# Order of loads, first steps, layer change and last tile in a two-layer conditioned attention kernel

## The chip, the cores and the metric

One core of a Trainium2 chip runs the whole program. The time is the device time of one execution in microseconds (us); the kernel before was timed three times: median 972.3 us, 969.69 to 973.74. Beside these stands one execution that was recorded by the hardware profiler.

## The reference, cut to what matters

Two layers of the same shape, in float32, on x of 32 tiles of 128 rows by 512 (32 sequences of 128 positions). Layer 0 has 16 heads of 32, layer 1 has 8 heads of 64:

```python
xn = layernorm(x) * norm_scale + norm_bias
q, k, v = xn @ Wq + bq, xn @ Wk + bk, xn @ Wv + bv
k = masked(k); v = masked(v)
q = softmax(q, over the features of a head)
k = softmax(k, over the 128 positions)
att = k^T v                      # per sequence and head
y = q @ att
scale, shift = split(silu(cond) @ W_film + b_film)      # one row per sequence
h = layernorm(y) * (1 + scale) + shift
x = x + silu(h) @ Wo + bo
```

## The kernel before, in words

**Tiles and products.** A tile is one sequence. There are NT = 64 tile steps: tiles 0 to 31 are layer 0, tiles 32 to 63 layer 1, and x stays in SBUF (X) between the layers. Every float32 product with a weight is made of three products of rounded operands: each operand is split into a high part (XH, HH, WH, made by ScalarE as a rounding copy) and a low part (XL, HL, WL, made by VectorE or POOL as the difference). `split_product` (line 663) makes four chunks of three matmuls each. A weight's split is `split_high` and `split_low` (lines 503 and 256), per chunk of 128 rows.

**One step s** (the loops over SLOTS, one on each engine) works on four tiles at once: tile i = s gets its keys, values and queries; tile j = s-2 its query transpose, attention and mix; tile o = s-3 its transposed y, FiLM and output product; and x for step m = s+2 is brought into place. Each engine runs its own list of these stages in the order that its loop writes, and waits on semaphores; no engine reorders. So the order of the work is written by hand.

**x into place.** For the first two pairs of tiles (g < FIRST = 2) VectorE normalises (`norm_x`), TensorE transposes (`turn_x`), and ScalarE applies norm scale and bias into XF and rounds it to XH (`x_turned`). For later pairs ScalarE normalises into XN (its own `norm_x`), VectorE transposes 32x32 blocks (`turn_blocks`, to XS), and SP writes XS to HBM (`x_turned`) and reads it back in another order as XT (`place_x`, one write and four reads). The keys go the same way: VectorE takes the maximum and the differences (`keys`), ScalarE the exponentials (`exp_k`), VectorE divides and transposes blocks (`normalise_keys`, `turn_keys`, to KT), and `place_keys` on SP writes a pair of tiles to HBM (`k_turned`) and reads it back to EK, on which `attention` waits. EK has one buffer, so its reads wait for the attention of the pair before.

**SP's queue** issues nearly all DMAs in one order, waiting where its code says: in step s the stores, the mask, x or key placing, x loads, FiLM weights and weights. The x loads are XLOADS (line 152): eight loads, the last two of eight tiles (2 MB) each, both issued in step 3. Their place in X holds layer 0's FiLM weights until then. The FiLM product of the condition runs in FILM_SLOTS = steps 1, 2, 6, 9, 12 and 15 on TensorE (`conditioning`, then `conditioning_fold`).

**Layer change.** Layer 1's weights are loaded chunk by chunk into STAGE, split, and put in place of layer 0's. SPLIT_MID, SPLIT_LATE and SPLIT_END (line 229) say in which step and where in it each is split; w = 4, 5, 6, 7 are its key, value, query and output weights. LOW_ON_DVE (line 228) says which chunks VectorE takes; POOL takes the rest. DRAIN (line 236) is the order after the last step.

The functions that the diff touches:

## Time and profile before

| what | value |
|---|---|
| timed runs, median | 972.3 us (969.69 to 973.74) |
| the profiled execution, its own time | 965.67 us |
| its span | 963.6 us |
| TensorE busy | 907.3 us (94%) |
| VectorE busy | 731.0 us (76%) |
| ScalarE busy | 591.0 us (61%) |
| POOL busy | 446.5 us (46%) |
| mean granted TensorE clock | 0.98 |

TensorE's busy time is close to the span, so what counts is where it is not busy. The span is the time from the first to the last record of the profile; the execution's own time holds 2.1 us more around it. The granted clock is a share of full speed. In the rows a dash arrow `X<-Y` means that X is written from Y, and the bracket at the end of a row gives the idle time before it and what ended it.

### The profile page before, as it was taken

The page shows a single profiled execution, that of the slowest core. Times are in us where ns is not written, and L with a number is a line of the kernel's source. Part 1 is how long each engine was busy: PE and PEld are TensorE (multiplying, and loading weights), DVE is VectorE, ACT ScalarE, POOL GpSimd, SP SyncE. Part 2 cuts the span into 40 slices and gives each one's busy share as a digit, 9 for nine tenths or more (in the row PEclk, how much of TensorE's full clock was granted, in tenths as well). Part 3 has the DMA queues.
Part 4 walks back from the last instruction along what each step waited for, and adds up shares of the span by engine and source line. Part 5 has one row for each costly group of instructions (what it writes and reads, how often), then busy time and mean ns, then how long its engine had stood idle before and what let it go on. Part 6 is the DMA issues. An engine that isn't in the chain of part 4 may idle for free.

```text
span 963.6 us, 20376 instructions
## 1 busy us (share of the span) xinstructions
PE 907.3 (94%) x7069; PEld 773.0 (80%) x7069; DVE 731.0 (76%) x1347; ACT 591.0 (61%) x1445; POOL 446.5 (46%) x624
## 2 busy tenths in 40 slices
PE   4877899999999999999979999999999999999986
PEld 3555788888888888888868888888888888888874
DVE  6756577778688788888778888787888887877654
ACT  4336455756666677666766667666766666666634
POOL 3444344544545455445555645444554454443320
PEclk9989799999999999999989999999999999999998
DMA  8738223423232223222254222233333223223110
GB/s 299 276 93 284 72 72 116 132 100 110 72 117 75 90 94 94 94 77 84 73 169 138 101 81 93 95 106 92 117 115 114 86 93 104 99 89 111 67 67 33
DMA packets 69915, 105.84 MB, mean 110 GB/s; under 512 B 6687, under 2 KB 46743, under 8 KB 69815
## 3 DMA queue, kind: packets, MB, share of 16 engines
q1 hardware_dynamic: 69312, 104.10, 32.3%
q8 instruction: 57, 0.93, 0.4%
q10 hardware_dynamic: 502, 0.46, 0.2%
q14 instruction: 44, 0.35, 0.1%
HBM read 63.63 MB, written 40.89 MB: 108 GB/s over the span
## 4 chain that ended last, share of the span: by engine, by line
PE 78%; DMA 8%; ACT 4%; DVE 4%; issue 3%; SPq 2%; POOL 0%; ACTq 0%; DVEq 0%
PE PS L670 64%; PE PS L750 5%; DMA k_turned<-KT 4%; PE PS L736 3%; PE PS L710 3%; PE PS L718 2%; DMA EK<-k_turned 2%; ACT SK L518 1%; ACT Z L538 1%; DMA x_turned<-XS 1%; DMA STAGE<-in_wk 1%; SPq L324 1%; PE PS L784 1%; ACT XF L589 1%; SPq L312 1%
## 5 line engine op out<-in xcount | busy, mean ns | idle before, releaser
L524 ACT ACTIVATE YN<-YN,NBY,RSY 128x512 f32<-128x512 f32 x64 | 52.1, 815 | 266.4 <-POOL NBY L426 266.4
L670 PE MATMUL PS<-XH,WH_k 128*128 128x256 f32 x512 | 146.6, 286 | 6.1 <-DVE XL L906 4.8
L670 PE MATMUL PS<-XH,WL_k 128*128 128x256 f32 x512 | 146.2, 286 | 0.0
L670 PE MATMUL PS<-XL,WH_k 128*128 128x256 f32 x512 | 146.2, 285 | 0.0
L400 POOL TENSOR_SCALAR VEY<-MVY 128x1 f32<-128x1 f32 x64 | 14.9, 233 | 260.1 <-DVE MVY L993 259.8
L445 POOL TENSOR_TENSOR SQ<-SQ,QM 128x512 f32<-128x512 f32 x64 | 67.2, 1051 | 99.0 <-DVE QM L954 98.5
L670 PE MATMUL PS<-WH_o,HH 128*128 128x512 f32 x256 | 107.7, 421 | 5.4 <-DVE HL L1005 3.4
L670 PE MATMUL PS<-WH_q,XH 128*128 128x512 f32 x256 | 108.9, 425 | 2.9 <-DVE WL_q L261 2.9
L670 PEld LDWEIGHTS PS<-XH,WH_k 128*128 128x128 f32 x512 | 99.5, 194 | 9.7 <-ACT XH L596 5.2
L670 PE MATMUL PS<-WH_v,XH 128*128 128x512 f32 x256 | 106.2, 415 | 0.0
L670 PE MATMUL PS<-WL_o,HH 128*128 128x512 f32 x256 | 102.5, 401 | 0.0
L670 PE MATMUL PS<-WH_o,HL 128*128 128x512 f32 x256 | 102.2, 399 | 0.0
L670 PE MATMUL PS<-WL_q,XH 128*128 128x512 f32 x256 | 101.6, 397 | 0.0
L670 PEld LDWEIGHTS PS<-XL,WH_k 128*128 128x128 f32 x512 | 99.5, 194 | 2.6
L670 PE MATMUL PS<-WH_q,XL 128*128 128x512 f32 x256 | 101.4, 396 | 0.0
L670 PE MATMUL PS<-WH_v,XL 128*128 128x512 f32 x256 | 100.4, 392 | 0.0
L670 PE MATMUL PS<-WL_v,XH 128*128 128x512 f32 x256 | 99.5, 389 | 0.0
L670 PEld LDWEIGHTS PS<-XH,WL_k 128*128 128x128 f32 x512 | 99.5, 194 | 0.0
L518 ACT ACTIVATE SK<-SK,KN 128x128 f32<-128x128 f32 x256 | 98.7, 387 | 0.0
L538 ACT ACTIVATE Z<-PS,FC,FA 128x128 f32<-128x128 f32 x256 | 96.2, 463 | 2.2 <-PE PS L718 2.2
L438 POOL TENSOR_TENSOR X<-X,BB 128x512 f32<-128x512 f32 x64 | 84.7, 1323 | 4.9
L454 POOL TENSOR_TENSOR XL<-XF,XH 128x512 fp32r<-128x512 f32 x60 | 77.6, 1294 | 19.7 <-ACT XH L596 19.7
(124 smaller groups left out, 2206.8 us busy)
## 6 DMA issues: line engine op xcount, KB each, us to landing
k_turned<-KT SPq DMA_DIRECT2D x32, 512.0 KB, 2.7
EK<-k_turned SPq DMA_DIRECT2D x128, 128.0 KB, 2.8
x_turned<-XS SPq DMA_DIRECT2D x30, 512.0 KB, 2.6
XT<-x_turned SPq DMA_DIRECT2D x120, 128.0 KB, 2.8
out_x<-X SPq DMA_DIRECT2D x32, 256.0 KB, 2.1
X<-in_film SPq DMA_DIRECT2D x2, 2048.0 KB, 17.1
X<-in_x SPq DMA_DIRECT2D x2, 2048.0 KB, 11.8
STAGE<-in_film SPq DMA_DIRECT2D x4, 1024.0 KB, 8.1
```

The costliest lines, as they stand in the source:

```text
L400: eng.tensor_scalar(plus, var, EPS, None, ALU.add).then_inc(pool_own, 1)
L438: eng.tensor_tensor(X[:, b, :], X[:, b, :], BB[:, 2, :], ALU.add).then_inc(pool_bo, 1)
L445: eng.tensor_tensor(sq, sq, QM[:, 0:D // w].unsqueeze(2).to_broadcast([P, D // w, w]), ALU.subtract)\
L454: eng.tensor_tensor(XL[g % 2][:, dst, :], XF[:, :, :], XH[g % 2][:, dst, :].bitcast(F32), ALU.subtract).then_inc(pool_xl, 1)
L518: e = eng.activation(SK[:, p, a, :], SK[:, p, a, :], ACT.Exp, bias=KN[:, t, cc:cc + 1], accum_out=SE[:, a:a + 1])
L524: eng.activation(YN[:, :], YN[:, :], ACT.Identity, bias=NBY[:, :], scale=RSY[:, :]).then_inc(act_yn, 1)
L538: z = eng.activation(Z[:, c * P:c * P + P], PS[:, B_TY, c * P:c * P + P], ACT.Identity, bias=FC[l][:, c, b:b + 1], scale=FA[l][:, c, b:b + 1])
L670: mm = eng.matmul(dst, left[a](c), right[b](c), start=(c == 0 and a + b == 0), stop=(c == C - 1 and a == 1))
L710: mm = eng.transpose(bank(B_TQ, c * P, P), SQ[j % 2][:, c * P:c * P + P], ident[:, :])
L718: mm = eng.transpose(bank(B_TY, c * P, P), YN[:, c * P:c * P + P], ident[:, :])
L736: mm = eng.matmul(PS[f:f + 32, B_ATT, c * P + a:c * P + a + w], vs if l == 0 else ks, ks if l == 0 else vs, start=True, stop=True, tile_po ...
L750: mm = eng.matmul(bank(B_Y + c // 2, (c % 2) * W, W), EQ[:, c * P:c * P + P], ATT[:, c // 2, (c % 2) * W:(c % 2 + 1) * W], start=True, sto ...
```

## The change: what it does

- XLOADS: tiles 16 to 31 come in eight loads of two tiles, one in each of steps 3 to 10, and these loads and the FiLM loads are issued behind `place_keys`. In step 1 x is placed before the keys.
- XF has two buffers, and the second half of a pair uses a PSUM bank of its own (B_Y) for its transposes; XN's halves are apart too. The waits of `x_turned`, `turn_x` and `norm_x` are loosened accordingly.
- Start: ScalarE turns both halves of x before it splits weights; keys(0) waits chunk by chunk; x of steps 2 and 3 is made in step 0; VectorE takes three of four chunks of the query weights (w = 2); `start_cond` moves behind values(0).
- Layer change: w = 4 is split at the end of step 31, w = 5 first in step 32, w = 6 at the end of step 32; queries(32) come last in step 32 on TensorE; the chunks are shared out anew.
- End: keys of tile 63 are made, normalised and placed in step 62.

```diff
@@ -79,7 +79,7 @@
         XT = sb("XT", [P, Q, 2, C, 32])
-        XF = sb("XF", [P, 2, PAIR])
+        XF = [sb(f"XF{n}", [P, 2, PAIR]) for n in range(2)]
         XH = [sb(f"XH{n}", [P, C, PAIR], F32R) for n in range(2)]
@@ -147,9 +147,10 @@
         B_ATT = B_XK
-        XLOADS = [(0, 1), (1, 1), (2, 2), (4, 4), (8, 4), (12, 4), (16, 8), (24, 8)]
+        B_X = [B_XK, B_Y]
+        XLOADS = [(0, 1), (1, 1), (2, 2), (4, 4), (8, 4), (12, 4)] + [(n, 2) for n in range(16, B, 2)]
         ld_x = [sem(f"ld_x{n}") for n in range(len(XLOADS))]
@@ -217,6 +218,10 @@
+        def keys_at(s):
+            return [NT - 1] if s == NT - 2 else []
         def block_turn_at(s):
@@ -225,8 +230,8 @@
-        LOW_ON_DVE = [range(C), range(C), [3], [], range(2), range(2, C), range(C), []]
-        SPLIT_MID, SPLIT_LATE, SPLIT_END = {31: [4], 32: [6]}, {31: [5]}, {1: [3], 34: [7]}
+        LOW_ON_DVE = [range(C), range(C), [1, 2, 3], [], range(2), range(3), range(2), []]
+        SPLIT_FIRST, SPLIT_LAST, SPLIT_END = {B: [5]}, {B - 1: [4], B: [6]}, {1: [3], 34: [7]}
         LAST_USE = {4: pe_k, 5: pe_v, 6: pe_q, 7: pe_o}
@@ -352,20 +357,8 @@
                     load_mask(eng, s // 2 + 1)
-                for g in block_turn_at(s) if s > 1 else []:
+                for g in block_turn_at(s):
                     place_x(g)
-                if s == 3:
-                    eng.wait_ge(pe_film, 2)
-                    load_x(6)
-                    load_x(7)
-                    wait_split(3)
-                for n in range(2, 6):
-                    if s == FILM_SLOTS[n - 1] + 1:
-                        eng.wait_ge(pe_film, n)
-                        load_film(n)
-                if s == FILM_SLOTS[-1] + 1:
-                    eng.wait_ge(pe_film, 6)
-                    load_w(4)
                 if s == B - 1:
@@ -375,10 +368,22 @@
                     load_w(7)
-                if s % 2 == 1:
+                if s % 2 == 1 and s < NT - 2:
                     place_keys(s // 2)
-                for g in block_turn_at(s) if s == 1 else []:
-                    place_x(g)
+                if s == NT - 2:
+                    place_keys(NT // 2 - 1)
+                if s == 3:
+                    eng.wait_ge(pe_film, 2)
+                    wait_split(3)
+                if 3 <= s < 11:
+                    load_x(s + 3)
+                for n in range(2, 6):
+                    if s == FILM_SLOTS[n - 1] + 1:
+                        eng.wait_ge(pe_film, n)
+                        load_film(n)
+                if s == FILM_SLOTS[-1] + 1:
+                    eng.wait_ge(pe_film, 6)
+                    load_w(4)
             for b in range(B - 4, B):
@@ -451,7 +456,7 @@
                 dst = slice(2 * p, 2 * p + 2)
-                eng.tensor_tensor(XL[g % 2][:, dst, :], XF[:, :, :], XH[g % 2][:, dst, :].bitcast(F32),
+                eng.tensor_tensor(XL[g % 2][:, dst, :], XF[p][:, :, :], XH[g % 2][:, dst, :].bitcast(F32),
                                   ALU.subtract).then_inc(pool_xl, 1)
@@ -473,6 +478,8 @@
                     queries(s - 1)
+                for w in SPLIT_FIRST.get(s, []):
+                    split_low(eng, w, low_on_pool(w))
                 if 2 * FIRST <= s + 2 < NSTEP:
@@ -480,7 +487,7 @@
                     mask_of_keys((s + 1) // 2)
-                for w in SPLIT_MID.get(s, []) + SPLIT_LATE.get(s, []):
+                for w in SPLIT_LAST.get(s, []):
                     split_low(eng, w, low_on_pool(w))
@@ -579,21 +586,20 @@
                     eng.wait_ge(dve_vec, 1)
-                wait_x_low(eng, m)
-                eng.wait_ge(act_xh, m)
+                wait_x_low(eng, m - 1)
                 for cc in range(2):
                     if g < FIRST:
-                        src = PS[:, B_XK, cc * PAIR:(cc + 1) * PAIR].rearrange("p (t q n) -> p t q n", t=2, q=Q)
+                        src = PS[:, B_X[p], cc * PAIR:(cc + 1) * PAIR].rearrange("p (t q n) -> p t q n", t=2, q=Q)
                     else:
                         src = XT[:, :, :, 2 * p + cc, :].rearrange("p q t n -> p t q n")
-                    f = eng.activation(XF[:, cc, :].rearrange("p (t q n) -> p t q n", t=2, q=Q), src, ACT.Identity,
+                    f = eng.activation(XF[p][:, cc, :].rearrange("p (t q n) -> p t q n", t=2, q=Q), src, ACT.Identity,
                                        bias=vec(l, "norm_bias", 2 * p + cc, 1),
...
                     eng.wait_ge(pe_q, 2 * g - 2)
-                eng.activation(XH[g % 2][:, 2 * p:2 * p + 2, :], XF[:, :, :], ACT.Copy).then_inc(act_xh, 1)
+                eng.activation(XH[g % 2][:, 2 * p:2 * p + 2, :], XF[p][:, :, :], ACT.Copy).then_inc(act_xh, 1)
@@ -608,9 +614,8 @@
             x_turned(0)
-            split_high(0, range(2))
             x_turned(1)
-            split_high(0, range(2, C))
+            split_high(0)
             split_high(1)
@@ -620,26 +625,34 @@
                     norm_y(o)
+                for w in SPLIT_FIRST.get(s, []):
+                    split_high(w)
                 if s in FILM_SLOTS:
                     conditioning_sums(FILM_SLOTS.index(s))
-                if m < NSTEP:
+                if s < 2:
+                    exp_k(i)
+                if s != 1 and m < NSTEP:
                     x_turned(m)
+                if s == 0:
+                    x_turned(m + 1)
                 if 0 <= j:
...
                     film(o)
-                exp_k(i)
+                if 2 <= s < NT - 1:
+                    exp_k(i)
                 if 0 <= j:
                     heads(j)
-                for w in SPLIT_MID.get(s, []):
-                    split_high(w)
                 if 0 <= o:
...
                 values(i)
-                if s > 0:
-                    for n in (norm_at(0) if s == 1 else []) + norm_at(s):
-                        norm_x(n)
-                for w in SPLIT_LATE.get(s, []) + SPLIT_END.get(s, []):
+                for w in SPLIT_LAST.get(s, []):
+                    split_high(w)
+                for n in keys_at(s):
+                    exp_k(n)
+                for n in norm_at(s):
+                    norm_x(n)
+                for w in SPLIT_END.get(s, []):
                     split_high(w)
@@ -666,6 +679,9 @@
                         eng.wait_ge(low_w[fresh][c], 1)
+                    if fresh == 0 and c % 2 == 0:
+                        eng.wait_ge(act_xh, c // 2 + 1)
+                        eng.wait_ge(dve_xl, c // 2 + 1)
                     for a, b in ((0, 0), (0, 1), (1, 0)):
@@ -675,8 +691,9 @@
                 l = i // B
-                eng.wait_ge(act_xh, 2 * g + 2)
-                wait_x_low(eng, 2 * g + 2)
+                if i > 0:
+                    eng.wait_ge(act_xh, 2 * g + 2)
+                    wait_x_low(eng, 2 * g + 2)
                 eng.wait_ge(dve_ka, i)
@@ -743,6 +760,8 @@
                 eng.wait_ge(dve_yr, j)
+                if j == 0:
+                    eng.wait_ge(act_xf, 2 * FIRST)
                 if j >= B:
@@ -763,11 +782,14 @@
             def turn_x(m):
+                g, p = divmod(m, 2)
                 eng.wait_ge(dve_xn, m + 1)
-                eng.wait_ge(act_xf, m)
+                if m >= 2:
+                    eng.wait_ge(act_xf, m - 1)
                 for cc in range(2):
                     for t in range(2):
-                        mm = eng.transpose(bank(B_XK, cc * PAIR + t * T, T), XN[:, t, cc * P:cc * P + P], ident[:, :])
+                        f = (2 * p + cc) * P
+                        mm = eng.transpose(bank(B_X[p], cc * PAIR + t * T, T), XN[:, t, f:f + P], ident[:, :])
                 mm.then_inc(pe_a, 1)
@@ -802,20 +824,19 @@
                 i, j, o, m = s, s - 2, s - 3, s + 2
-                if 0 <= i < NT:
+                if s < NT - 1:
                     keys(i)
...
                     conditioning(FILM_SLOTS.index(s))
-                if 0 <= j < NT:
+                if 0 <= j:
                     turn_queries(j)
-                if 0 <= o < NT:
+                if 0 <= o:
                     turn_y(o)
-                if 0 <= i < NT:
-                    values(i)
-                if 0 <= j < NT:
+                values(i)
+                for n in keys_at(s):
+                    keys(n)
+                if 0 <= j:
                     attention(j)
-                if 1 <= s and m < 2 * FIRST:
-                    turn_x(m)
                 if s == 0:
@@ -824,11 +845,11 @@
                     conditioning_fold(FILM_SLOTS.index(s))
-                if 0 <= i < NT:
+                if s != B:
                     queries(i)
                 if s == 0:
-                    turn_x(m)
-                if s == 0:
+                    turn_x(2)
+                    turn_x(3)
@@ -837,10 +858,12 @@
                     mm.then_inc(pe_cond, 1)
-                if 0 <= j < NT:
+                if 0 <= j:
                     mix(j)
-                if 0 <= o < NT:
+                if 0 <= o:
                     output(o)
+                if s == B:
+                    queries(i)
             for stage, n in DRAIN:
@@ -879,11 +902,13 @@
                 eng.wait_ge(pool_x, 2 * g + 2)
-                eng.wait_ge(pe_a, m)
+                if g > 0:
+                    eng.wait_ge(pe_a, m - 1)
                 for t in range(2):
...
                     r = n % RING
-                    ins = eng.tensor_scalar(XN[:, t, 0:2 * P], X[:, n % B, 2 * p * P:2 * (p + 1) * P], MVX[:, r, 0:1],
+                    f = slice(2 * p * P, 2 * (p + 1) * P)
+                    ins = eng.tensor_scalar(XN[:, t, f], X[:, n % B, f], MVX[:, r, 0:1],
                                             RSX[:, r:r + 1], ALU.subtract, ALU.mult)
@@ -903,7 +928,7 @@
                 dst = slice(2 * p, 2 * p + 2)
-                eng.tensor_tensor(XL[g % 2][:, dst, :], XF[:, :, :], XH[g % 2][:, dst, :].bitcast(F32),
+                eng.tensor_tensor(XL[g % 2][:, dst, :], XF[p][:, :, :], XH[g % 2][:, dst, :].bitcast(F32),
                                   ALU.subtract).then_inc(dve_xl, 1)
@@ -1082,57 +1107,65 @@
             x_low(0)
-            split_low(eng, 0, range(2))
             x_low(1)
-            split_low(eng, 0, range(2, C))
+            split_low(eng, 0, range(C))
             start_masks()
...
             stat_x(3)
-            start_cond()
+            split_low(eng, 2, LOW_ON_DVE[2])
+            norm_x(2)
+            norm_x(3)
             for s in SLOTS:
...
                     queries(s - 1)
-                if 0 < s and m < 2 * FIRST:
-                    norm_x(m)
+                for w in SPLIT_FIRST.get(s, []):
+                    split_low(eng, w, LOW_ON_DVE[w])
                 for g in block_turn_at(s) if s > 1 else []:
                     turn_blocks(g)
-                keys(i)
+                if s < NT - 1:
+                    keys(i)
                 if s == 0:
-                    split_low(eng, 2, LOW_ON_DVE[2])
                     values(i)
-                    norm_x(m)
                     start_valid()
+                    start_cond()
+                    x_low(2)
+                    normalise_keys(i)
                     start_count()
+                    x_low(3)
                 for n in stats_at(s):
...
                     h_mul(o)
-                for w in SPLIT_MID.get(s, []):
-                    split_low(eng, w, LOW_ON_DVE[w])
                 if s > 0:
...
                     second_ones()
-                normalise_keys(i)
+                if 0 < s < NT - 1:
+                    normalise_keys(i)
                 if 0 <= o:
                     h_low(o)
-                if m < 2 * FIRST:
-                    x_low(m)
+                for w in SPLIT_LAST.get(s, []):
+                    split_low(eng, w, LOW_ON_DVE[w])
                 if s in FILM_SLOTS:
                     conditioning(FILM_SLOTS.index(s))
-                turn_keys(i)
+                if s < NT - 1:
+                    turn_keys(i)
+                for n in keys_at(s):
+                    keys(n)
                 if 0 <= j:
                     mixed(j)
+                for n in keys_at(s):
+                    normalise_keys(n)
+                    turn_keys(n)
                 if s == 1:
...
                     turn_blocks(g)
-                for w in SPLIT_LATE.get(s, []) + SPLIT_END.get(s, []):
+                for w in SPLIT_END.get(s, []):
                     split_low(eng, w, LOW_ON_DVE[w])
...
```

## Rows read from the trace of the kernel before

**Rows 1.** Stretches view, a step each: bounds, length, busy times, clock, DMA.

```profile
core 0: us, PE busy (x) PEld busy (x) DVE busy (x) ACT busy (x) POOL busy (x), PEclk, DMA share, GB/s
322.18:335.71 13.53, 13.53 (x110) 11.68 (x108) 10.06 (x19) 8.93 (x22) 5.84 (x10) 1.00 0.21 51
...
29.34:46.79 17.45, 13.80 (x78) 9.43 (x77) 11.59 (x25) 8.60 (x26) 8.24 (x13) 0.90 0.72 265
...
46.79:67.08 20.29, 14.36 (x117) 11.16 (x117) 10.37 (x19) 9.40 (x22) 9.95 (x10) 0.88 0.37 111
...
67.08:83.41 16.33, 14.95 (x111) 12.69 (x111) 14.69 (x28) 8.81 (x22) 7.72 (x13) 0.94 0.45 143
...
83.41:110.20 26.79, 16.34 (x110) 13.73 (x108) 10.14 (x19) 9.03 (x22) 5.88 (x10) 0.75 0.56 193
...
470.98:489.73 18.75, 15.32 (x110) 12.88 (x109) 15.15 (x25) 13.61 (x31) 14.73 (x16) 0.91 0.45 155
...
489.73:507.38 17.65, 15.05 (x110) 12.75 (x108) 12.19 (x23) 11.19 (x26) 5.17 (x8) 0.90 0.40 127
```

**Rows 2.** The waits of TensorE: line, waited for, us in total, times, longest.

```profile
PE PS L736 <- DMA EK<-k_turned: 16.5, 5, 10.5
```

**Rows 3.** Timeline of TensorE: start, length, what, idle before it.

```profile
34.88 3.62 PE L784 MATMUL PS<-X,CT 128*32 128x512 f32 x16 [2.40 <-DVE SQ L950]
...
46.79 0.36 PE L670 MATMUL PS<-XH,WH_k 128*128 128x256 f32 x1 [1.24 <-issue]
...
65.33 2.10 PE L750 MATMUL PS<-ATT,EQ 128*128 128x132 f32 x8 [5.51 <-issue]
...
100.50 0.66 PE L736 MATMUL PS<-EK,VV 128*32 128x32 f32 x32 [10.45 <-DMA EK<-k_turned]
...
160.36 0.46 PE L736 MATMUL PS<-EK,VV 128*32 128x32 f32 x32 [1.35 <-DMA EK<-k_turned]
...
245.89 0.46 PE L736 MATMUL PS<-EK,VV 128*32 128x32 f32 x32 [0.77 <-DMA EK<-k_turned]
...
485.30 0.60 PE L670 MATMUL PS<-WH_o,HH 128*128 128x512 f32 x1 [3.43 <-DVE HL L1005]
...
499.36 0.77 PE L670 MATMUL PS<-WH_q,XH 128*128 128x512 f32 x1 [2.60 <-DVE WL_q L261]
...
937.64 0.65 PE L736 MATMUL PS<-VV,EK 128*32 128x64 f32 x32 [3.21 <-DMA EK<-k_turned]
...
943.55 2.10 PE L750 MATMUL PS<-ATT,EQ 128*128 128x132 f32 x8 [2.75 <-ACT ATT L557]
```

**Rows 4.** Chain of waits in step 3, issuing queue: start, length, what.

```profile
79.26 3.91 SPq L293
...
83.22 12.96 DMA k_turned<-KT
```

**Rows 5.** List of DMA issues: how many, KB each, us to landing.

```profile
k_turned<-KT SPq DMA_DIRECT2D x32, 512.0 KB, 2.7
...
EK<-k_turned SPq DMA_DIRECT2D x128, 128.0 KB, 2.8
```

**Rows 6.** The timeline of ScalarE, POOL and VectorE in the first steps.

```profile
12.07 1.15 ACT L509 ACTIVATE WH_k<-STAGE 128x512 fp32r<-128x512 f32 x2 [1.83 <-DMA STAGE<-in_wk]
...
19.62 4.22 POOL L261 TENSOR_TENSOR WL_q<-X,WH_q 128x512 fp32r<-128x512 f32 x3 [10.00 <-ACT WH_q L509]
...
21.05 1.64 DVE L1061 SCALAR_TENSOR_TENSOR KT<-Z,KT 32x512 f32<-32x512 f32 x1
...
76.81 0.69 DVE L998 SCALAR_TENSOR_TENSOR H<-H,Z 128x512 f32<-128x512 f32 x1 [0.44 <-ACT H L543]
```

**Rows 7.** The timeline of POOL at the layer change.

```profile
481.71 2.94 POOL L261 TENSOR_TENSOR WL_k<-STAGE,WH_k 128x512 fp32r<-128x512 f32 x2
```

**Rows 8.** The timeline of TensorE and ScalarE in step 62.

```profile
916.40 1.06 PE L750 MATMUL PS<-ATT,EQ 128*128 128x132 f32 x8
...
920.79 0.81 ACT L524 ACTIVATE YN<-YN,NBY,RSY 128x512 f32<-128x512 f32 x1 [5.11 <-POOL NBY L426]
...
923.40 0.60 PE L718 MATMUL PS<-ident,YN 128*128 128x128 f32 x4
```

More of the change, by code:

```diff
@@ L1175 @@
         arrays[f"film{l}"] = g["film"]
-    nc = bacc.Bacc("TRN2", target_bir_lowering=False, num_devices=1, dynamic_dma_scratch_size=4096)
+    nc = bacc.Bacc("TRN2", target_bir_lowering=False, num_devices=1, dynamic_dma_scratch_size=2048)
     arrays = {f"in_{k}": np.ascontiguousarray(v) for k, v in arrays.items()}
```

## Prediction

> **What bounds the kernel now.** I read the stretches view by step first. A step is the time from one tile's first key matmul to the next one's. In an undisturbed step of layer 0 TensorE is busy 13.53 us out of 13.53, so nothing that other engines save there can show; only lost TensorE time can be won back [rows 1]. Against those 13.53 us, steps 1 to 4 take 17.45, 20.29, 16.33 and 26.79 us, and the two steps at the layer change 18.75 and 17.65 us [rows 1]. Next came TensorE's waits. Waiting for the read-back of placed keys (EK) costs 16.5 us in five places, 10.5 of it in one [rows 2]. Then each idle stretch by time, with what ended it [rows 3]: the 10.45 us before the attention of step 4, 5.51 us before a mix in step 2, 3.43 and 2.60 us at the layer change, 3.21 and 2.75 us at the end. Last, the chain of waits around the largest: SP issues two x loads (eight tiles, 2 MB each), a 1 MB FiLM load at 79.26, and only at 83.22 the key write, which takes 12.96 us to land [rows 4]; the read-back that follows it ended the wait at 100.50. The usual landing times are 2.7 us for the write and 2.8 us for a read-back part [rows 5].
>
> **Step 4 (late x loads behind the placing): 13.3 us.** The two x loads and the FiLM load of step 3 move behind the key write and read-back. Key write to attention was 83.22 to 100.50, 17.3 us. With nothing ahead it is 2.7 (write) + 1.8 (four issues at about 0.43) + 2.8 (landing) = 7.3 us [rows 5]. By the order of VectorE's work, KT should be turned about 8.5 us before the attention is due, so I expect 1 us of slack and no wait. Step 4 falls from 26.79 to 13.53, or 13.3 us: the 10.45 us wait and 2.8 us that the same work took longer at the lower clock (mean granted 0.75 in that step) [rows 1, 3]. Cover gone means a stall of up to 4 us: bounds 9 to 13.3. The eight pieces add six issues on SP of 0.43 us each; their data is first read in step 11 and SP has idle time in each step, so I cost them at nothing; if placings wait behind them see the rivals.
>
> **Steps 8 and 14: 2.1 us.** FiLM loads issued in steps 7 and 13 now also come after the placing; they preceded EK waits of 1.35 and 0.77 us [rows 3]. Bounds 0 and 2.1. The wait of 0.7 us in step 34, the rest of the five, follows the load of layer 1's output weights, whose place ahead of the keys is unchanged; it stays.
>
> **First steps: 3.3 us.** I followed each queue in the new order.
> Step 0: the second half of x no longer waits for the first (own XF, own bank) nor stands behind two weight chunks, and each weight chunk releases its own three matmuls. WH_k starts at 12.07 [rows 6]; plus 0.6 and 0.7 the first matmul goes at about 13.5, 2.1 us earlier than 15.62. Taking two of POOL's three WL_q chunks (4.22 us for three [rows 6]) to VectorE ends the queries 3 us earlier. None of it is carried on: VectorE still reaches keys(0) at 24.4, since two statistics, three WL_q chunks and two normalisations stand in front, and TensorE's keys(1) stands behind start_cond, at about 27.1 + 1.4 + 0.7 = 29.2, against 29.34 [rows 1].
> start_cond took 1.64 us for its first instruction while POOL ran; the same form on 128 partitions takes 0.69 elsewhere [rows 6]. It is now clear of POOL's chunk, so I take 0.69 twice, 1.4; at the old price, bound 3.4, keys(1) would be 2.0 us later.
> The Trainium skill (GPSIMD Engine Reference, Specifications) says that GpSimd and VectorE share SBUF interfaces and contend when a VectorE instruction has two SBUF inputs. By it the sum is the 1.4 one; without it, the 3.4 one.
> Step 1: the FiLM matmuls waited until 34.88 for VectorE's queries(0) [rows 3]. The new queue puts an x_low, the count and both statistics before it: about 35.7, 0.8 us lost. Then turn_x(3) (0.45 us) is gone, and so is the 1.24 us wait for the XL of step 2 [rows 3]: keys(2) at 46.0, 0.8 ahead.
> Step 2: XN is ready early, so XS is turned at 46.8. SP now writes x first: 46.8 + 2.7 + 1.8 = 51.3 for the key write, + 2.7 + 1.8 + 2.8 = 58.6 for EK. The attention, due at 54.2, waits 4.4 us; ScalarE has x in time, so the 5.51 us wait of the mix is replaced by it, not removed. The rest of the step (5.1 us) plus 1.7 us of lower clock puts keys(3) at 65.4, 1.7 ahead of 67.08.
> Step 3: no cold start, but YN after the late mix still comes a microsecond late: 14.7 to 14.9 against 16.33, 1.4 to 1.6 more. Sum 3.3. Below, if start_cond and VectorE's queue run later, -1; above, if step 2's wait goes as well, 8.
>
> **Layer change: 3.6 us.** In step 31 ScalarE's four WH_k chunks move behind h_high, which removes the 3.43 us wait for HL [rows 3]. POOL's two WL_k chunks (2.94 us [rows 7]) end near 485.0, in time for the fourth chunk of keys(32), which starts at 484.7 instead of 489.73: 5.0 won. In step 32 two waits are new. The WL_v split stands first: with POOL's chunk after its queries, values(32) ends at 492.5, 1 us late. The key write still stands behind four value-weight loads and a bias on SP (485.9, as before), so EK lands at 494.7 and the attention waits 2.2 us. ScalarE then owes a split, x, exp, FiLM and exp before the copy of ATT (496.9), so the mix waits 1.7 us more and the output 0.4 us. Queries(32), now last, find WL_q ready (2.60 us wait [rows 3] gone). Keys(33) at 503.8 against 507.38: 3.6. Both steps at 13.53 would give 9.3 [rows 1]; ScalarE or POOL 4 to 5 us later than I reckon would give -1.
>
> **End: 1.0 us.** keys(63) in step 62 lets EK be written early; the read-back waits only for the attention of step 61, so the 3.21 us wait goes [rows 3]. What is late next is POOL's queries(63). Moving 2.9 us of keys from between the mix and the next turn_y to before the mix costs: mix at 916.40, YN at 920.79 + 0.81 = 921.6, 5.2 us later; a mix at 919.3 gives YN at 924.5 where TensorE is there at 923.4: 1.1 lost [rows 8]. With all that the last mix starts at 942.9 instead of 943.55, 0.6 won. It runs at the low clock now (2.10 us [rows 3]); I add 0.4 for a shorter cold part. Bounds -1 and 4.
>
> **Sum**: 13.3 + 2.1 + 3.3 + 3.6 + 1.0 = 23.3 us. The profiled execution had a span of 963.6 and a time of 965.7, so it would come to 940.3 and 942.4. The median of the timed runs is 972.3, 6.6 above it; I subtract from that: 949.0.
>
> **Rivals.**
> (A) The forecast, 949.0, own range 943 to 955: chance 0.55.
> (B) The layer change is hidden fully: 9.3 instead of 3.6, so 943.3; all upper bounds together (13.3 + 2.1 + 8 + 9.3 + 4 = 36.7) give 935.6. For it: TensorE alone needs 13.53 a step. Against: the key write behind the value weights. Chance 0.2.
> (C) The reordering is a wash and only the DMA order pays: 15.4, so 956.9. For it: VectorE is busy 14.69 us of step 3's 16.33 and 15.15 of step 31's 18.75 [rows 1], and each reorder adds work before something. Chance 0.15.
> (D) It doesn't do what it says: each piece delays a placing as a FiLM load did, 1.35 us in eight steps, 10.8, and the 2.1 isn't won either: 972.3 - 23.3 + 12.9 = 961.9. Against: each piece is issued after the read-back and has most of a step to land. Chance 0.06.
> (E) The other side. In steps 3, 5, 7 and 9 a piece, twice with a FiLM load, and then the next piece follow the read-back at once. If the engines share out between them, at the 2.6 us a MB that the key write's 12.96 us behind 5 MB shows [rows 4], 2 MB make EK some 5 us late, and each such stall costs 2.8 us of low clock more: 4 x 7.8 = 31, so 980. It decides from 3.0 us late in each of the four, 4 x 5.8 = 23.3. Against: the FiLM load of step 10 is already issued behind a read-back, and step 10 shows no wait. Chance 0.04.
> For (E) the Trainium skill (DMA: Bandwidth & Descriptors, Queues, rings and completion order) says that descriptors of one issuing engine's ring are consumed in ring order, and round-robin is between rings; all these come from SP. By that rule the later loads would not slow the read-back; by sharing, the time would be 980.
>
> **How the numbers follow.** Faster by over 0.5% (4.9 us, about what a measurement of this kernel can tell): A, B, C, D, 0.96 less a little for all of them shrinking: 0.95. Same 0.02, slower 0.03. The range leaves out (D), (E) and the far end of (B): 938 to 958.
>
> **What would show it.** Right: step 4 at 13.5 to 14.5 us and no EK wait over 1 us in steps 4 to 14; the first key matmul at 13.5 and keys(1) still at 29; an EK wait of about 4 us in step 2 in place of the mix's; keys(32) 13.7 us after keys(31), then a 19 us step with EK and ATT waits; no EK wait after step 63. Wrong: step 4 over 17 us, an EK wait in each even step up to 10, or both steps of the layer change at 13.6.

## The result, and the profile after

The changed kernel took 944.75 us, median of 4 runs (942.48 to 946.47), beside 971.0 us (964.75 to 973.74) for the kernel before: a ratio of 0.9737, interval 0.9684 to 0.979, so 2.7% faster. The profiled execution has a span of 943.2 us and a time of 944.95, so between the two profiles 20.4 us went. When both were run again the ratio was 0.978 (0.9754 to 0.9806). The kernel before had medians of 967.25 to 968.59 us in three later sets of nine runs, so its four runs here lie high, and a gain of 22 to 24 us, 2.2 to 2.5%, is the better figure.

A stretch's bounds are the first key matmuls of two tiles. The stretches by step of the changed kernel (stretch, its length, busy time and instructions of PE, PEld, DVE, ACT and POOL, granted clock, DMA share, GB/s): steps 1 to 4, 8 and 14, then 31, 32 and 34, and the end from step 62 on. They answer to [rows 1].

```profile
28.79:43.59 14.80, 13.82 (x73) 11.20 (x73) 12.73 (x28) 7.09 (x17) 8.28 (x13) 0.82 0.88 323
43.59:65.78 22.19, 16.64 (x117) 12.99 (x116) 10.67 (x19) 9.14 (x21) 10.04 (x10) 0.77 0.32 101
65.78:81.06 15.28, 14.08 (x111) 11.82 (x110) 13.42 (x24) 8.81 (x22) 7.62 (x12) 1.00 0.32 105
81.06:94.59 13.53, 13.53 (x110) 11.68 (x108) 10.08 (x19) 8.93 (x22) 5.93 (x10) 1.00 0.65 205
136.75:150.75 14.00, 13.59 (x109) 11.68 (x108) 10.06 (x19) 8.93 (x22) 5.87 (x10) 1.00 0.62 200
221.90:235.41 13.51, 13.51 (x110) 11.66 (x109) 10.08 (x19) 8.92 (x22) 5.90 (x10) 1.00 0.41 128
453.55:467.08 13.53, 13.53 (x110) 11.68 (x108) 12.54 (x22) 11.01 (x26) 9.63 (x11) 1.00 0.34 105
467.08:488.35 21.27, 16.89 (x110) 13.94 (x108) 14.94 (x27) 14.15 (x31) 11.24 (x16) 0.84 0.58 175
501.87:515.58 13.71, 13.71 (x110) 11.83 (x108) 10.16 (x23) 8.93 (x22) 5.79 (x10) 1.00 0.17 50
886.49:943.20 56.71, 44.15 (x353) 36.21 (x351) 29.57 (x54) 26.01 (x61) 11.04 (x19) 0.96 0.17 56
```

Step 4 is an undisturbed step now: 13.53 against 26.79. Step 31 is whole too, and step 32 is longer than the 17.65 it took. Step 2 grew from 20.29 to 22.19. The waits of TensorE (us in total, times, longest) answer to [rows 2]:

```profile
PE PS L753 <- DMA EK<-k_turned: 9.1, 3, 5.6
PE PS L735 <- ACT YN L531: 4.6, 5, 1.5
PE PS L769 <- ACT ATT L564: 2.8, 1, 2.8
```

EK fell from 16.5 us in five waits to 9.1 in three. The idle stretches of TensorE (start, length, instruction, idle time before it and its releaser) say where, beside [rows 3]:

```profile
13.48 0.55 PE L686 MATMUL PS<-XH,WH_k 128*128 128x256 f32 x1 [3.86 <-DVE WL_k L266]
35.26 1.92 PE L806 MATMUL PS<-X,CT 128*32 128x512 f32 x16 [0.98 <-DVE SQ L975]
57.38 0.66 PE L753 MATMUL PS<-EK,VV 128*32 128x32 f32 x32 [5.55 <-DMA EK<-k_turned]
143.82 0.46 PE L753 MATMUL PS<-EK,VV 128*32 128x32 f32 x32 [0.41 <-DMA EK<-k_turned]
477.87 0.61 PE L753 MATMUL PS<-EK,VV 128*32 128x32 f32 x32 [3.13 <-DMA EK<-k_turned]
905.19 0.66 PE L735 MATMUL PS<-ident,YN 128*128 128x128 f32 x4 [1.45 <-ACT YN L531]
919.13 0.66 PE L727 MATMUL PS<-ident,SQ 128*128 128x128 f32 x4 [1.23 <-POOL SQ L450]
924.03 1.14 PE L769 MATMUL PS<-ATT,EQ 128*128 128x132 f32 x8 [2.75 <-ACT ATT L564]
```

The waits of [rows 3] at 100.50, 245.89, 485.30, 499.36 and 937.64 have no counterpart. In their place stand 5.55 us before the attention of step 2 (where the mix had waited 5.51), 3.13 us before that of step 32, and short ones at the end (the 2.75 us before the last mix was there before).

### The profile page after: what moved, and what is told of

The parts are those of the page before. It is cut to its first block, busy times and chain, and to the rows that moved or that the text cites. A ratio compares the mean times of both kernels' runs of the same rounds, so it can differ in the third digit from the quotient of the medians.

```text
span 943.2 us, 20349 instructions
## 1 busy us (share of the span) xinstructions
PE 904.5 (96%) x7069; PEld 772.6 (82%) x7069; DVE 729.0 (77%) x1348; ACT 591.2 (63%) x1445; POOL 444.1 (47%) x623
## 4 chain that ended last, share of the span: by engine, by line
PE 87%; DMA 4%; DVE 3%; ACT 2%; issue 2%; SPq 1%; POOL 1%; DVEq 0%; ACTq 0%; POOLq 0%
PE PS L686 71%; PE PS L769 6%; PE PS L753 3%; PE PS L735 3%; PE PS L727 3%; DMA X<-in_x 1%; DMA k_turned<-KT 1%; DMA EK<-k_turned 1%; PE PS L806 1%; ACT Z L545 1%; ACT SK L525 0%; PE PS L815 0%; SPq L329 0%; SPq L288 0%; ACT YN L531 0%
## 5 line engine op out<-in xcount | busy, mean ns | idle before, releaser
L459 POOL TENSOR_TENSOR XL<-XF,XH 128x512 fp32r<-128x512 f32 x60 | 77.6, 1293 | 15.8 <-ACT XH L602 15.6
```

What stands on the lines that cost most here:

```text
L459: eng.tensor_tensor(XL[g % 2][:, dst, :], XF[p][:, :, :], XH[g % 2][:, dst, :].bitcast(F32), ALU.subtract).then_inc(pool_xl, 1)
```

## The experiments

In the expectations "changed" is the changed kernel. Each diff is against it unless it says otherwise. The kernel before, run beside them, had a median of 968.59 (e1 to e4), 967.76 (e5 to e8) and 967.25 us (e11, e12), nine runs each.

**e1: the DMA order alone.** The kernel before, with one part of the change. (One line that belongs to no part differs too between the kernel before and the changed one with all its versions, and in e1: `dynamic_dma_scratch_size` is 2048 instead of 4096. No run varies it alone. In e3, with 2048, the wait of step 4 is there, and in e1 the start, the layer change and the end take what they take in the three profiles of the kernel before, within 0.2 us of one of them each, so nothing points to it.)

```diff
-XLOADS = [..., (16, 8), (24, 8)]
+XLOADS = [...] + [(n, 2) for n in range(16, B, 2)]
-                # x loads, FiLM loads and load_w(4) between place_x and place_keys
                 place_keys(s // 2)
+                # ... the same ones here; one load_x a step
```

> The kernel before, with only the order of loads changed: eight loads of two tiles in steps 3 to 10, and these and the FiLM loads behind the key placing; step 1, the start, the layer change and the end stay as before. Theory (the late loads alone remove the stall of step 4): step 4 falls from 26.8 to 13.5 us, steps 8 and 14 give 1.8 to 2.1 more, the rest stays; 15.0 to 15.4 us less than the kernel before in the profile, span about 948. Rival (parts help each other: the stall goes only since the first steps also end earlier): step 4 keeps an EK wait of 2 us or more, and the gain is under 11 us.

It took 950.32 us: ratio 0.9815 (0.9789 to 0.984), span 948.0. Its stretches of steps 4, 31 and 32:

```profile
81.33:94.84 13.51, 13.51 (x109) 11.67 (x108) 10.08 (x19) 8.92 (x22) 5.87 (x10) 1.00 0.65 205
453.62:471.99 18.37, 14.95 (x110) 12.62 (x108) 15.23 (x25) 13.58 (x30) 14.55 (x15) 0.93 0.48 158
471.99:490.10 18.11, 15.51 (x109) 13.17 (x108) 12.12 (x23) 11.33 (x26) 5.45 (x9) 0.88 0.39 124
```

The theory's span of about 948 came, and no EK wait is left in step 4. Step 4 is mended with the start, the layer change and the end as they were. So this part carries 18.3 of the gain in medians, and the rest of the change 5 to 6 us.

**e2: two loads of eight tiles, behind the placing.**

```diff
-XLOADS = [...] + [(n, 2) for n in range(16, B, 2)]
+XLOADS = [..., (16, 8), (24, 8)]
-                if 3 <= s < 11:
-                    load_x(s + 3)
+                if s == 3:
+                    load_x(6)
+                    load_x(7)
```

> The changed kernel, but tiles 16 to 31 come again in two loads of eight tiles, both issued in step 3 behind the key placing. Theory (the place in the queue counts, the size doesn't): no EK wait in step 4 and a span within 1 us of 943.2, or up to 3 us more if the 5 MB (two loads and FiLM) are still moving when step 5 writes x. Rival (DMAs of one queue share the engines, so what is issued behind a read-back slows it): EK lands late in step 4, an EK wait of 5 us or more there, span 950 or more.

It took 944.85 us: 0.9758 (0.9737 to 0.978). Steps 4 and 5, and then SP's queue (issue time, its length), in two fences:

```profile
82.22:95.72 13.50, 13.50 (x109) 11.66 (x108) 10.08 (x19) 8.92 (x22) 5.87 (x10) 1.00 0.88 279
95.72:109.25 13.53, 13.53 (x109) 11.69 (x108) 11.91 (x21) 8.92 (x22) 7.65 (x11) 1.00 0.78 269
```

```profile
82.56 1.73 SPq L329 DMA_DIRECT2D EK<-k_turned  x4
84.46 1.02 SPq L283 DMA_DIRECT2D X<-in_x  x2
85.52 4.69 SPq L298 DMA_DIRECT2D STAGE<-in_film  x1
```

Four megabytes issued within 2 us of the read-back leave both steps undisturbed: its four parts landed in a median of 2.9 us, as against 2.8 as a rule [rows 5]. The place in the queue counts, not the size of the loads, and rival (E), that the engines share out between them, falls.

**e3: the loads ahead again, the rest of the change kept.**

```diff
-XLOADS = [...] + [(n, 2) for n in range(16, B, 2)]
+XLOADS = [..., (16, 8), (24, 8)]
                     place_x(g)
+                # load_x(6), load_x(7), the FiLM loads and load_w(4) here
                 ...
                 place_keys(s // 2)
-                # ... and no longer here
```

> The changed kernel with the loads where they were: two loads of eight tiles and the FiLM load ahead of the key placing of step 3, the later FiLM loads ahead of theirs; all else of the change kept. Theory (terms add up): the 13.3 us of step 4 and the 1.8 of steps 8 and 14 come back, span 943.2 + 15 = 958. Rival (the other parts hide part of the stall, or the stall grows since keys are ready earlier while the loads take as long): a span of 952 or less, or 961 or more.

It took 963.41 us: 0.9945 (0.9924 to 0.9965), span 960.4. The attention of steps 4, 8 and 14:

```profile
98.14 0.66 PE L753 MATMUL PS<-EK,VV 128*32 128x32 f32 x32 [10.76 <-DMA EK<-k_turned]
158.38 0.46 PE L753 MATMUL PS<-EK,VV 128*32 128x32 f32 x32 [2.62 <-DMA EK<-k_turned]
245.58 0.60 PE L753 MATMUL PS<-EK,VV 128*32 128x32 f32 x32 [2.45 <-DMA EK<-k_turned]
```

The wait of 10.45 us is back, and step 4 takes 26.22 us. The span lies between the theory's 958 and the rival's 961: step 4 cost 12.7 us (13.3 in the theory), but steps 8 and 14 cost 6.3 instead of 1.8, with waits longer than the 1.35 and 0.77 of [rows 3]. That is no effect of the other parts, since the kernel before has waits of 2.02 and 2.56 there in e9: their price is no constant.

**e4: the key write parted from its read-back,** and put ahead of the x placing in step 1 and of the value weights in step 31.

```diff
+            def write_keys(g): ...      # the wait for KT and the write
-            def place_keys(g):
+            def place_keys(g, write=True):
+                if s == 1:
+                    write_keys(0)
                 place_x(g)
                 if s == B - 1:
+                    write_keys(s // 2)
                     load_w(5)
-                    place_keys(s // 2)
+                    place_keys(s // 2, s not in (1, 31))
```

> The changed kernel with the write of the keys parted from their read-back on the issuing queue in two steps: in step 1 the key write goes ahead of the placing of x, in step 31 ahead of the load of the value weights; the read-backs stay where they are. Theory (both remaining EK waits come from the write standing behind other DMAs, and each costs its wait and then low clock): step 2 falls from 22.2 to about 16.5 us, the wait of 5.6 us going to 1 or less and its low clock with it; step 32 from 21.3 to about 17 us; span about 933. Rival (another wait takes the place of each: ScalarE's copy of ATT in step 32, x for ScalarE in step 2): the EK waits go but an ATT wait of 2 us or more stands behind them, and the span stays over 939.

It took 941.79 us: 0.9726 (0.9701 to 0.9751), span 938.8. Steps 1, 2 and 32, and TensorE's waits in them:

```profile
28.21:45.00 16.79, 14.56 (x75) 11.05 (x74) 12.71 (x29) 7.33 (x17) 7.81 (x13) 0.80 0.82 301
45.00:61.81 16.81, 14.78 (x117) 11.43 (x116) 10.66 (x18) 9.14 (x21) 10.04 (x10) 0.90 0.43 134
463.40:484.32 20.92, 16.42 (x109) 13.39 (x108) 15.20 (x27) 14.95 (x33) 12.09 (x16) 0.84 0.62 188
```

```profile
55.26 0.46 PE L761 MATMUL PS<-EK,VV 128*32 128x32 f32 x32 [2.03 <-DMA EK<-k_turned]
472.90 0.66 PE L761 MATMUL PS<-EK,VV 128*32 128x32 f32 x32 [1.09 <-DMA EK<-k_turned]
475.68 2.10 PE L777 MATMUL PS<-ATT,EQ 128*128 128x132 f32 x8 [2.12 <-issue]
```

In step 2 the EK wait falls by 3.5 us and the step by 5.4, of which step 1 gives back 2.0 in this execution. In a second one (e12) step 1 took 14.81 us and step 2 18.81: the two together 33.6 in both, against 37.0 and 38.6 in the changed kernel's two profiles. In step 32 the EK wait falls by 2.0 and the step only by 0.35 (in e12 by nothing, 21.38 us): the mix now waits 2.12 us, where it had waited 0.75. By ScalarE's timeline its copy of ATT ends just before the mix starts. So the theory held for steps 1 and 2 and the rival for step 32.

**e5: the start as before.** Steps 0 and 1 get back x behind the keys, the order of splits and turns, the place of `start_cond`, and the query weights' chunks; the buffers stay two. The diff is cut.

```diff
-LOW_ON_DVE[2] = [1, 2, 3]
+LOW_ON_DVE[2] = [3]
-                if s != 1 and m < NSTEP: x_turned(m)
-                if s == 0: x_turned(m + 1)
+                if m < NSTEP: x_turned(m)
+                if s == 1: turn_x(3)        # first on TensorE in step 1
```

> The changed kernel with the first steps as in the kernel before: order of steps 0 and 1 on all engines, x behind the keys in step 1, shares of the query weights. Late loads, layer change and last tile as changed. Theory (the first steps are worth little or nothing; most of the 2.35 us by which step 4 starts earlier was that one conditioning product ran at the full clock): step 4 starts within 1.5 us of the changed kernel's 81.1, span 943 to 945, timed the same within 2 us. Rival (the 3.3 us of the prediction are real): step 4 starts at 83.4 or later and the kernel is 2.3 to 3.3 us slower than the changed one.

It took 944.4 us: 0.9756 (0.9732 to 0.9781), span 942.5. Steps 1, 2 and 3:

```profile
28.86:44.61 15.75, 12.08 (x78) 9.16 (x77) 11.59 (x25) 8.59 (x26) 8.26 (x13) 1.00 0.81 299
44.61:64.24 19.63, 14.34 (x116) 11.16 (x117) 10.36 (x19) 9.41 (x22) 9.95 (x10) 0.90 0.37 114
64.24:80.58 16.34, 15.46 (x110) 13.17 (x110) 14.70 (x28) 8.81 (x22) 7.73 (x13) 0.91 0.28 98
```

Step 4 starts at 80.58, no later than in the changed kernel (81.06), and the medians agree within 0.8 us: the theory was right. The reordered start is worth nothing that this run could show. The kernel before itself starts step 4 at 81.43 in e9, so if the first steps gained anything, the second buffers, which e5 keeps, may have given it; no run has them alone.

**e6: the layer change as before.**

```diff
-LOW_ON_DVE[5], LOW_ON_DVE[6] = range(3), range(2)
+LOW_ON_DVE[5], LOW_ON_DVE[6] = range(2, C), range(C)
-SPLIT_FIRST, SPLIT_LAST = {B: [5]}, {B - 1: [4], B: [6]}
+SPLIT_MID, SPLIT_LATE = {31: [4], 32: [6]}, {31: [5]}
-                if s == B:
-                    queries(i)              # last in step 32
```

> The changed kernel with the weight splits of steps 31 and 32 and the queries of tile 32 in the places of before. Theory (what step 31 wins, step 32 gives back in waits for EK and ATT and in low clock): steps 31 and 32 take 36.4 together against 34.8, and step 34 some 14.5 against 13.7; 1.6 to 2.4 us slower than the changed kernel. Rival (with the keys ready early anyway the new order costs nothing extra): 3.6 us slower or more.

It took 949.3 us: 0.9803 (0.9779 to 0.9826), 4.5 us over the changed kernel's median. Steps 31, 32 and 34:

```profile
453.60:472.25 18.65, 15.24 (x109) 12.89 (x108) 15.13 (x25) 13.60 (x30) 14.72 (x16) 0.91 0.48 156
472.25:491.71 19.46, 16.18 (x110) 13.63 (x108) 12.20 (x23) 11.54 (x26) 5.18 (x8) 0.82 0.37 115
505.23:520.57 15.34, 13.79 (x110) 11.83 (x108) 10.20 (x23) 9.04 (x22) 5.80 (x10) 1.00 0.32 98
```

Steps 31 and 32 take 38.11 instead of 34.80 (the theory had 36.4), and step 34 gets back the wait that I had forecast to stay in it. The loss of 4.1 to 4.5 us, by which of the changed kernel's medians is taken, is the rival's "3.6 or more".

**e7: the keys of tile 63 in their own step.**

```diff
-            return [NT - 1] if s == NT - 2 else []
+            return []
-                if s < NT - 1: keys(i)
+                keys(i)
 ...              # exp_k, normalise_keys, turn_keys and place_keys likewise
```

> The changed kernel with the keys of tile 63 in step 63 as before. Theory (the 3.2 us EK wait comes back, the 1.45 us wait for YN in step 63 goes, and the rest of the end follows POOL's queries and the low clock): 0.5 to 1 us slower, span 943.7 to 944.2. Rival (the early keys help by the whole wait): 3 us slower. Third (early keys cost more than they save): faster by 0.5 us or more.

It took 947.01 us: 0.9792 (0.976 to 0.9824); in the profile the end takes 57.48 instead of 56.71. The span is 0.9 us over the changed kernel's, as in the theory; the median is 1.8 to 2.3 over it, one of the four runs being at 952.29, so the size stays between theory and rival. The end's stretch, and the wait that is back, in two fences:

```profile
886.62:944.10 57.48, 45.10 (x353) 37.95 (x351) 29.64 (x54) 25.78 (x61) 10.74 (x19) 0.94 0.16 56
```

```profile
917.94 0.98 PE L751 MATMUL PS<-VV,EK 128*32 128x64 f32 x32 [3.25 <-DMA EK<-k_turned]
```

**e8: x for step 34 behind the split in step 32,** on top of e4, with VectorE taking all four low chunks of w = 6.

```diff
-LOW_ON_DVE[6] = range(2)
+LOW_ON_DVE[6] = range(C)
-                if s != 1 and m < NSTEP:
+                if s not in (1, B) and m < NSTEP:
                     x_turned(m)
                     split_high(w)
+                if s == B:
+                    x_turned(m)
```

> The kernel of the parted key writes (steps 1 and 31), and in step 32 ScalarE turns x of tile 34 behind the split of the query weights instead of ahead of the exponentials, and VectorE takes all four low chunks of the query weights. Theory (ScalarE's queue ahead of the ATT copy is what bounds step 32 once EK is early): ATT is copied 1.5 us earlier, the mix waits 1 us or less, step 32 falls from 20.9 to about 18 us, span 935.5 to 937. Rival (VectorE takes over as the bound, with the low chunks, the keys and the mix of the same step): the ATT wait shrinks but queries(32) or the YN of step 33 waits instead, step 32 and 33 together within 1 us of 34.4.

It took 941.87 us: 0.9731 (0.9707 to 0.9755), no better than e4. Within step 32:

```profile
470.00:476.40 6.40, 3.71 (x44) 2.46 (x45) 5.86 (x13) 5.97 (x19) 1.28 (x1) 0.95 1.09 296
476.40:481.00 4.60, 4.59 (x15) 4.01 (x16) 3.58 (x7) 4.27 (x8) 0.00 (x0) 0.50 0.37 133
```

```profile
470.43 0.47 PE L696 MATMUL PS<-WH_v,XH 128*128 128x512 f32 x1 [1.43 <-DVE WL_v L266]
476.41 2.10 PE L779 MATMUL PS<-ATT,EQ 128*128 128x132 f32 x8 [1.13 <-issue]
```

The wait for ATT falls from 2.12 to 1.13 us, nearly as forecast, but the first value matmul waits 1.43 us for WL_v instead of 0.51, and what follows runs at 0.50 of the clock. Nothing that the edit moves stands ahead of that wait. ScalarE's own row shows that it stood idle 0.97 us for the load of the value weights before its first chunk, which it had not in e4; and in e12, e4's kernel again, the wait for WL_v is 1.00 us.

```profile
468.86 1.88 ACT L524 ACTIVATE WH_v<-STAGE 128x512 fp32r<-128x512 f32 x3 [0.97 <-DMA STAGE<-in_wv]
```

Steps 32 and 33 take 34.54 us together, the number of the rival; its cause, VectorE as the bound, isn't shown. In the first stretch ScalarE is busy 5.97 and VectorE 5.86 us of 6.40, so neither has room there.

**e9, e10: the kernel before, twice more,** for how much its own steps vary; no edit.

> The kernel before once more, profiled, to see where its timed runs, 962 to 974 us, differ from its first profiled one (965.7, span 963.6). Theory (the waits behind loads vary from run to run): the EK waits of steps 4, 8, 14 and 34, 10.5, 1.4, 0.8 and 0.7 us in the first profile, come out 3 us or more apart from these in sum when the span is 966 or more; steps 17 to 30 at 13.53 us as ever. Rival (the low clock in the first steps and the layer change varies instead): these waits agree within 1 us and steps 0 to 3 or 31 to 32 carry the difference.

> The same kernel a third time, with the same expectations, since one more profile may fall on either end of its spread.

They took 968.44 and 966.66 us (spans 966.7 and 964.9). Step 4 took 25.83 and 26.74 us. Steps 8, 14 and 34 of the first of the two:

```profile
149.42:165.04 15.62, 13.60 (x110) 11.68 (x108) 10.11 (x19) 9.02 (x22) 5.80 (x10) 1.00 0.22 64
236.15:253.84 17.69, 15.13 (x109) 12.84 (x108) 10.13 (x19) 9.03 (x22) 5.88 (x10) 0.90 0.26 85
522.06:537.35 15.29, 13.83 (x109) 11.83 (x108) 10.21 (x23) 9.03 (x22) 5.80 (x10) 1.00 0.29 98
```

The same steps took 14.99, 14.34 and 14.53 us in the first profile. Most undisturbed steps repeat to 0.03 us; those behind a load don't. The EK waits of steps 4, 8, 14 and 34 sum to 16.9 us in e9, 3.6 more than in the first profile, with a span of 966.7: the theory held.

**e11, e12: the changed kernel and e4's kernel again,** side by side.

> The changed kernel once more, on the chip and in the rounds of the next run. Theory (its first profile is typical): step 4 starts at 80.5 to 82.5, steps 31 and 32 take 34.3 to 35.1, 13 and 14 take 27.4, median 943 to 946. Rival: one of these lies outside, and the parts as read from one profile are off by as much.

> The parted key writes once more, beside the changed kernel. Theory (the gain is the 5.4 us of step 2 less some low clock in step 1): 2.5 to 5 us faster than the changed kernel in the same rounds. Rival (low clock elsewhere gives it all back): within 1 us of it.

They took 945.17 (944.1 to 946.25; 0.978, 0.9754 to 0.9806) and 943.39 us (940.95 to 943.9; 0.9762, 0.9736 to 0.9787). All four numbers expected of e11 came: step 4 starts at 82.29, steps 31 and 32 take 34.92, steps 13 and 14 27.35. The parted key write gains 1.8 us in medians (3.0 when e4 is set against the changed kernel's 944.75) and 5.3 between the two profiled spans, 944.5 and 939.2. The gain of medians lies between e12's theory (2.5 to 5) and its rival (within 1), and the two ratios' intervals overlap: it is the fastest version run, by too little to be sure of its size.

## Why the prediction was right

949.0 was forecast and 944.75 measured, inside the range. Of the rivals, (C) gave 956.9 and (B) 943.3, which is nearer the measured time than the forecast is; the rows below tell them apart where the time alone can't. Each line of the table takes all profiled executions with the old arrangement of that part, and all with the new one (for the first steps the start of step 4, for the others their lengths). In the three lines with six executions, the versions with the key write moved (e4, e8, e12) are left out:

| part | old | new | gain | forecast |
|---|---|---|---|---|
| step 4 | 26.4 (4 executions) | 13.5 (10) | 12.9 | 13.3 |
| steps 8, 13, 14 | 45.4 (4) | 41.4 (10) | 4.0 | 2.1 |
| first steps | 82.0 (5) | 81.4 (6) | 0.6 | 3.3 |
| steps 31 + 32 | 37.1 (5) | 34.6 (6) | 2.4 | 3.6 |
| step 34 | 14.8 (5) | 13.7 (9) | 1.1 | 0 |
| end from step 62 | 57.8 (5) | 56.5 (6) | 1.3 | 1.0 |
| sum | | | 22.3 | 23.3 |

The medians of e11 and of the kernel before beside it are 22.1 us apart. The sum came close in part by luck: the first steps gave 2.7 us less than forecast, steps 8 and 14 gave 1.9 more, and step 34 gave 1.1 that I had not counted.

**Step 4: right in size and cause.** e1 takes the wait away with no other part of the change, e3 brings it back with all others kept, and the changed kernel shows no EK wait over 0.5 us in steps 4 to 14 in either profile.

On the queue, the Trainium skill (DMA: Bandwidth & Descriptors, Queues, rings and completion order) says that on each DMA engine the descriptors of a ring are consumed in ring order. e2 agrees: 4 MB right behind the read-back cost it nothing, where 5 MB right ahead of the key write cost 10 us [rows 4].

**First steps: the term that was mis-sized, 0.6 instead of 3.3 us.** Every wait came where the working had put it: the first key matmul at 13.48 (13.5 forecast), keys(1) at 28.79 (29.2), and an EK wait in step 2 in place of the mix's. The step that failed is the one that priced what follows this wait: "the rest of the step (5.1 us) plus 1.7 us of lower clock". Two stretches of step 2, the wait and what comes after it:

```profile
51.83:57.38 5.55, 0.00 (x1) 0.01 (x1) 1.56 (x3) 3.74 (x12) 4.10 (x6) 0.76 0.49 138
57.38:65.78 8.40, 8.40 (x60) 7.18 (x61) 1.72 (x5) 1.91 (x3) 0.85 (x1) 0.55 0.06 10
```

The rest took 8.40 us and not 6.8 (8.23 in e11), at a mean granted clock of 0.55, which is nearly all of it at 1.2 GHz. The old wait stood at the step's end, before the mix, with 1.75 us of step 2 behind it [rows 1, 3]; the new one has queries and mix behind it. The wait was also 5.55 and not 4.4 us, and step 3 took 15.28 and not 14.7 to 14.9. In e11 keys(2) start at 45.33, 0.7 us earlier than the forecast's 46.0, and then step 2 takes 21.70 where 19.4 was forecast: what was mis-sized is step 2, in two executions.

The first two profiles show 2.35 us of gain here (step 4 at 83.41 and 81.06), but most of that is no gain of the change. The FiLM product of step 1 took 3.62 us in the first profile [rows 3] and 1.92 in the one after. Where it is slow, in either arrangement, step 1 is 1.6 to 2.1 us longer. The stretch of step 1 ahead of the product, in the changed kernel's first profile and in e11:

```profile
28.79:35.26 6.47, 5.49 (x26) 5.22 (x26) 5.95 (x15) 3.30 (x6) 1.85 (x5) 0.58 1.05 387
28.43:35.27 6.84, 4.63 (x26) 4.45 (x25) 5.94 (x15) 3.67 (x6) 1.84 (x5) 0.75 1.05 384
```

In both the product starts when VectorE is done, at 35.26 and 35.27. In the first more of the low clock (0.58) fell ahead of that moment, where TensorE had time to spare, and the wait was 0.98 us; in e11 less of it did, the wait was 2.21, and the product itself ran slow. Like with like, step 4 starts at 81.43 (e9) and 81.33 (e1) against 80.7 to 81.1 in the new order where the product took 1.92, and at 83.41 and 83.32 (e10) against 82.22 (e2) and 82.29 (e11) where it took 3.4 to 3.6: 0.3 to 1.2 us. Against e5 (80.58, product 1.92) there is none.

VectorE's first start_cond instruction ran without POOL at 0.67 us:

```profile
26.48 0.67 DVE L1086 SCALAR_TENSOR_TENSOR KT<-Z,KT 32x512 f32<-32x512 f32 x1
```

The second took 0.67 too. So 1.4 and not 3.4 us was the right end of that bound, and keys(1) came where 1.4 puts them. The rule of the Trainium skill on shared SBUF interfaces (GPSIMD Engine Reference, Specifications) agrees with it.

**Layer change: 3.5 came, by another sum.** Step 31 won all it could, 13.53 as against 13.7 forecast. Step 32 took 21.27 us instead of some 19: the EK wait was 3.13 instead of 2.2, and the 8.35 us from 480.0 to the step's end had a clock of 0.71. TensorE's idle time in the step was 4.4 us (21.27 less 16.89 busy) and the forecast's some 5.6, so the waits were not the miss: the same matmuls took 16.89 instead of 13.53 us. I had priced no low clock behind a wait that I had forecast myself. What made the sum whole is step 34, whose wait I had forecast to stay, since its weights' place in SP's queue is unchanged. It went in all nine executions with the new layer change and came back in e6:

```profile
513.43 0.65 PE L749 MATMUL PS<-VV,EK 128*32 128x64 f32 x32 [1.54 <-DMA EK<-k_turned]
```

SP's queue in step 33 shows how. The output weights go out right behind the read-back of x in both arrangements. But the write of x before it started 3.45 us into the step and landed in 4.0 to 5.0 us in the five executions with the old layer change, and started at 2.85 and landed in 2.7 to 3.1 in the nine with the new one; the read-back of the keys went out at 16.2 to 17.4 us and at 14.2 to 15.6. Why the write of x lands later in the old arrangement is open.

**Steps 8 and 14: right in kind, 4.0 instead of 2.1,** because the one execution that I priced them from had short waits: 14.99 and 14.34, against 15.62 and 17.69 in e9. Step 8 keeps an EK wait of 0.2 to 1.0 us in eight of nine executions with pieces, and has none in e2 and e12. The pieces are not shown to make it: e12 has them too. What goes with it is the landing of the key write, 3.9 us in e2 and e12, 4.4 in the changed kernel (wait 0.41) and 4.8 in e5 (wait 1.04), with no load in SP's queue between the read-back of x and it.

**End: right.** The EK wait before the attention went and the forecast YN wait of 1.1 came with 1.45. POOL's queries(63) are next with 1.23 us, and the 2.75 us for ATT stayed as it was.

**The median.** Profile to profile 23.3 us were forecast and 20.4 measured. The time itself came out 4.2 us lower than forecast, since I carried 6.6 us from one profiled execution to a median of three runs; the nine-run medians of the kernel before are 967.3 to 968.6, 1.6 to 2.9 us above that execution. That the measured time came so near (B)'s 943.3 is this offset and no hidden layer change: steps 31 and 32 took 34.6 us, where (B) has 27.

## What to carry to other kernels

Ask of each large load what small, urgent transfer stands behind it in the same queue, and issue it after that one: this order was worth 18 of the 22 to 24 us, and cutting the loads up nothing that e2 could show. Where a forecast leaves a wait of some microseconds on TensorE, price the matmuls behind it at the low clock, and look how many there are before the next stage: here moving a wait from a step's end to its middle made it dearer. Don't price a wait behind a load, or a step that may fall to the low clock, from one execution; take two or three profiles of the kernel before.

## What was not expected of the hardware

The waits behind one and the same load vary from run to run: step 8 took 14.51 to 15.62 us and step 14 14.34 to 17.69 in three profiles of the kernel before, while steps 17 to 30 all took 13.5 us (one of them 13.80). After waits of 3 to 6 us TensorE ran stretches of up to 8.4 us at about half of the clock. In step 1 a 2.2 us wait came before the slow FiLM product in e2, e4, e8 and e11, but 2.40 before the slow one of the first profile and 2.39 before the fast one of e9: the length of the wait alone doesn't say whether it falls.
